# A two-layer attention and expert kernel: TensorE's groups of the first attention stage in another order

## The reference

```
x = x + _L0_xattn_ref(_layernorm(x), ctx, ctx, layer_indices, mask, ...)
q = split_heads(query @ Wq.T + bq) / sqrt(16)
k = split_heads(key @ Wk.T + bk)
v = split_heads(value @ Wv.T + bv)
scores = einsum('bhqd,bhkd->bhqk', q, k) + (1 - mask) * NEG
scores = where(same_layer_index, scores, NEG)
attn = softmax(scores)
ctx = einsum('bhqk,bhkd->bhqd', attn, v)
out = ctx @ Wo.T + bo
```

## Time and profile before

| what | value |
|---|---|
| median of three runs | 1462.81 us (1456.46 to 1464.56) |
| profiled execution: span | 1453.1 us |
| the runs above that span | 3.4 to 11.5 us, the median 9.7 |
| busy share of the span: TensorE matmuls, VectorE, ScalarE, GpSimd | 92%, 60%, 57%, 47% |
| first attention stage, b = 1 to 29, on TensorE's row | 33.08 to 350.39 us |

### The profile page before, as it was taken

The page is one execution under the profiler, slowest core; times in us unless marked ns, Lnnn a source line. Parts: engine busy times, 40 slices in busy tenths (PEclk is TensorE's granted clock), DMA queues, the critical chain, the costliest instruction groups (busy, mean ns, idle before and its releaser), DMA issues.

```text
span 1453.1 us, 37961 instructions
## 1 busy us (share of the span) xinstructions
PE 1337.7 (92%) x13114; PEld 1095.2 (75%) x13114; DVE 866.1 (60%) x2396; ACT 825.9 (57%) x1945; POOL 680.5 (47%) x939
## 2 busy tenths in 40 slices
PE   6999999997779999999997899999974999999997
PEld 5787777775546666666665799999963989889896
DVE  4787777877643333333332688888874666666664
ACT  4787777776345555555553566666643445444443
POOL 4235455455553333333331558778745344444323
PEclk8999999998789999999999899999996999999999
DMA  4344333332159999999996233333213433333331
GB/s 146 95 127 117 101 105 114 99 98 68 34 111 181 204 181 173 178 178 178 178 178 142 77 92 89 91 102 95 88 56 73 128 124 124 126 122 108 121 110 53
DMA packets 280922, 172.99 MB, mean 119 GB/s; under 512 B 213054, under 2 KB 259360, under 8 KB 280740
## 3 DMA queue, kind: packets, MB, share of 16 engines
q1 hardware_dynamic: 259156, 135.85, 39.6%
q0 software_dynamic: 18608, 32.21, 7.9%
q10 hardware_dynamic: 2976, 2.52, 0.6%
HBM read 93.44 MB, written 31.97 MB: 86 GB/s over the span
## 4 chain that ended last, share of the span: by engine, by line
PE 81%; DMA 4%; issue 4%; DVE 4%; ACT 3%; POOL 2%; another core or an unknown queue 1%; SPq 0%; ACTq 0%; DVEq 0%; POOLq 0%
PE psum L2424 14%; PE psum L1495 12%; PE psum L1475 12%; PE psum L2441 7%; PE psum L1996 3%; PE psum L901 2%; PE psum L1986 2%; PE psum L830 2%; PE psum L843 2%; PE psum L804 2%; PE psum L918 2%; PE psum L882 2%; PE psum L904 2%; PE psum L1906 2%; PE psum L1945 2%
## 5 line engine op out<-in xcount | busy, mean ns | idle before, releaser
L2424 PE MATMUL psum<-d_xT,d_w 128*128 128x256 f16 (+1 forms) x2304 | 228.7, 256 | 0.0
L2424 PEld LDWEIGHTS psum<-d_xT,d_w 128*128 128x128 f16 x2304 | 199.3, 98 | 19.0
L1395 DVE SCALAR_TENSOR_TENSOR b_h<-b_hid,b_h 128x1024 f16<-128x1024 f32 x71 | 87.0, 1225 | 211.2 <-ACT b_h L1430 207.9
L1475 PE MATMUL psum<-arena,b_xT 128*128 x852 | 197.2, 382 | 9.6 <-DMA b_xT<-b_x 7.9
L1495 PE MATMUL psum<-arena,b_hT 128*128 x1704 | 197.7, 273 | 3.4 <-DMA b_hT<-b_h 3.4
L1495 PEld LDWEIGHTS psum<-arena,b_hT 128*128 128x128 f16 x1704 | 166.0, 98 | 39.1 <-issue 5.7
L1305 POOL DMA_INDIRECT b_xg<-dram_normed,b_gi x71 | 69.6, 981 | 200.7 <-issue 128.3
L1475 PEld LDWEIGHTS psum<-arena,b_xT 128*128 128x128 f16 x852 | 83.7, 98 | 98.5 <-issue 14.8
L2505 ACT ACTIVATE d_sg<-psum 128x256 f32<-128x256 f32 (+1 forms) x192 | 66.0, 348 | 146.6 <-PE psum L2424 136.5
L2566 DVE SCALAR_TENSOR_TENSOR d_hf<-psum,d_sg 128x256 f32<-128x256 f32 (+1 forms) x192 | 71.1, 379 | 104.0 <-ACT d_sg L2505 85.9
L1423 ACT ACTIVATE b_hid<-psum 128x512 f32<-128x512 f32 x142 | 83.6, 596 | 67.5 <-PE psum L1475 59.6
(11 more groups left out here) (328 smaller groups left out, 3014.7 us busy)
## 6 DMA issues: line engine op xcount, KB each, us to landing
d_wst<-in_L_w SPq DMA_DIRECT2D x64, 384.0 KB
stage<-in_L_w SPq DMA_DIRECT2D x32, 512.0 KB
dram_expert_rows<-b_ys SPq DMA_DIRECT2D x71, 128.0 KB
ctxT<-in_ctxT SPq DMA_DIRECT2D x64, 128.0 KB
dram_normed<-xn SPq DMA_DIRECT2D x64, 128.0 KB
x<-in_x SPq DMA_DIRECT2D x32, 128.0 KB, 5.1
dram_x<-xnew SPq DMA_DIRECT2D x32, 128.0 KB
c_x<-dram_x SPq DMA_DIRECT2D x32, 128.0 KB
```

The costliest lines, as they stand in the source:

```text
L1395: dve.scalar_tensor_tensor(out=h16[:, p, 1, :], in0=hid[:, p, :], scalar=H_SCALE, in1=h16[:, p, 0, :], op0=ALU.mult, op1=ALU.subtract).the ...
L1475: i = pe.matmul(psum[:, 1 + 2 * p + half, :], xT[:, j % NT, px, c, :], weights(e, c, pw, half * 512, 512), start=(n == 0), stop=(n == len( ...
L2424: i = pe.matmul(psum[:, q, m * n:(m + 1) * n], w16[:, fc % RING, pw, col:col + P], xT[:, p, px, c, at:at + n], start=(k == 0), stop=(k == ...
```

## The change

`project_kv` is split in `project_k` and `project_v`. All the waits of `project_kv` stay with `project_k`, the signal `kv_done` with `project_v`. In TensorE's loop `project_k(b + 2)` moves ahead of `scores_t(b)`; `transpose_x1(b - 3)` moves ahead of `values(b - 1)`; `count` and `logits(b - 3)` move ahead of `transpose_x(b + 2)` and `transpose_back(b - 1)`. On ScalarE `x2T_out(b - 3)` moves ahead of `pvT_out(b - 1)`. Lines behind the split move by three: L904 becomes L907, L911 L914, L918 L921, L932 L935, L941 L944.

```diff
--- before.py
+++ after.py
@@ -751,8 +751,8 @@
                     k_out(b + 1)
                     v_out(b + 1)
                     q_out(b + 1)
+                    x2T_out(b - 3)
                     pvT_out(b - 1)
-                    x2T_out(b - 3)
                     high(b)
                     xnT_out(b + 2)
                     mT_out(b)
@@ -883,7 +883,7 @@
-                def project_kv(b):
+                def project_k(b):
                     if inside(b):
                         pe.wait_ge(ctx_ld[b % 2], nth(b))
                         if b == 0:
@@ -900,6 +900,9 @@
                             for c in range(DC):
                                 pe.matmul(psum[:, 1, o * P:(o + 1) * P], wk[:, c, o * P:(o + 1) * P], ctxT[:, b % 2, c, :],
                                           start=(c == 0), stop=(c == DC - 1))
+
+                def project_v(b):
+                    if inside(b):
                         for c in range(DC):
                             i = pe.matmul(psum[:, 1, 256:512], ctxT[:, b % 2, c, :], wv[:, c, :], start=(c == 0), stop=(c == DC - 1))
                         i.then_inc(kv_done, 1)
@@ -971,22 +974,23 @@
                 for b in range(-3, NB + 6):
                     scores(b)
+                    transpose_x1(b - 3)
                     values(b - 1)
-                    transpose_x1(b - 3)
                     unseen(b - 1)
-                    transpose_x(b + 2)
-                    transpose_back(b - 1)
                     if last_of(b - 4) is not None:
                         count(last_of(b - 4), b - 3)
                     logits(b - 3)
+                    transpose_x(b + 2)
+                    transpose_back(b - 1)
                     if b == NB:
                         turn_pe(pe, 0)
                         turn_pe(pe, 1)
                     if b in (NB + 1, NB + 2):
                         turn_pe(pe, b - NB + 1)
                     transpose_m(b)
+                    project_k(b + 2)
                     scores_t(b)
-                    project_kv(b + 2)
+                    project_v(b + 2)
                     transpose_o(b - 1)
                     if b == -2:
                         values_bias()
```

## The result

The changed kernel took 1479.62 us (median of four runs, 1473.86 to 1486.38); the kernel before, in four runs beside it, 1463.68. The ratio is 1.0132, 95% interval 1.0106 to 1.0157: 19 us slower by the ratio (the two medians lie 16 apart), where 27 were forecast. The profiled executions differ by 24.8 us in span.

The account below looks back on a forecast made before the run. TensorE's matmuls, busy for 92% of a 1453.1 us span, were taken as the bound. The terms summed to 27.4 us, a span of 1480.5; with the median run 9.7 us above the span, 1490 us was forecast, range 1480 to 1502.

Parts of the forecast that it names:

- the two ends: Start and end of the stage: 0.5 us added for each.
- The bound, and what pays for a wait: First attention stage: TensorE idles only some 14 us, so any wait added to it is paid almost one for one.
- The k projection leaves the cover: Before `project_o`, b = 1 to 28: less work hides ScalarE's exps and `attT`, a new wait of 0.88 us each.
- The wait for `mT` goes: Inside `scores_t`: `project_k` covers the wait, winning 0.17 us in early iterations and 0.04 later.
- A wait ahead of `project_k`: Between `transpose_m` and `project_k`: waits for `top` of some 0.2 us, or for `cnt_read` of 0.49 with a count.
- Rows ahead of values: On TensorE and ScalarE: the new order makes nothing wait, costed at nothing; without ScalarE's idle time, 0.27 us an iteration.
- The five longer iterations: b = 12, 16, 20, 24, 28: their longer period may take in the new waits, 0.4 us each, 2.0 together.
- More time at the lower clock: Rival: added TensorE idle time drops the clock in seven more iterations, 11.6 us on top, 1502 us; chance 0.08.
- The waits ahead of `project_k` do not show: Rival: `top` is through in time for `project_k`, taking off about 6 us, 1484 us; chance 0.08.
- Faster: Rival: ScalarE's exps could start 0.9 us earlier, so no wait before `project_o`, 4 us won, 1459 us; chance 0.03.

Follow-up runs that it names:

- e1: Changed kernel with only the split and the move of `project_k` kept, rows, values, logits and ScalarE's order put back; 1460.91 us, ratio 1.0231 to the kernel before.
- e8: Changed kernel with `project_v` moved ahead of `scores_t` as well; 1482.43 us, ratio 1.0383 to the kernel before.
- e11: Kernel before with `project_q` moved ahead of `scores_t`, `xnT_out` ahead of `high`, `attT` still after the fourth exp; 1442.71 us, ratio 1.0079 to the kernel before.
- e3: Changed kernel with `transpose_o` right behind `scores_t` and `attT` evicted after the second exp; 1428.98 us, ratio 1.0000 to the kernel before.
- e7: Kernel before with `transpose_o` right behind `scores_t` and `attT` evicted after the second exp; 1442.65 us, ratio 1.0087 to the kernel before.
- e2: Changed kernel with `project_kv` whole again at its old place, the new order of rows, values and logits kept; 1429.13 us, ratio 1.0000 to the kernel before.
- e10: Kernel before with `project_q` ahead of `scores_t`, then `project_k`, `transpose_o`, `project_v`, `attT` after the third exp, `xnT_out` ahead of `high`; 1422.11 us, ratio 0.9945.

## Why the prediction was right, point by point

**The number.** Its direction and its main term are shown below; that the size came out so close is in part luck. The span was forecast as 1480.5 us and is 1477.9. But of its growth, 24.8 us for the 27.4 forecast, the stage has 16.7 where the sum had 26.4, and the two ends have 3.5 and 4.6 where it had 0.5 each. With 0.5 and 0.1 at the ends on the experiments' chip, the change does not explain those 8 us. The other 8 us between 1490 and 1479.62 are the step from span to run: I carried over the 9.7 us by which the median run of before lay above its profiled span, and the median changed run lies 1.7 us above its own.

**The bound, and what pays for a wait.** Right on the experiments' chip, where the stage's growth is 29.2 of the 29.8 us between the spans; in the first pair it is 16.7 of 24.8. "Almost one for one" holds for the period, not for idle time, since 6.0 of those 29.2 us are recorded as busy time.

**The k projection leaves the cover, 0.88 us.** Right in place and mechanism, shown by e1 (all of the loss), e8 (twice the cover taken, 0.92 us more idle time), e11 (another group taken, the same 0.61 us) and e3 beside e7 (the wait taken away, the loss gone). Its size was 0.78 us and not 0.88, since `project_v` takes 0.97 from start to start when it follows `scores_t` and so covers more; 0.11 us come back at the next `scores`, since `project_o` comes without overlap after its wait. That is 0.89 together.

**The wait for `mT` goes, 0.17 early and 0.04 later.** Mis-sized: 0.55 in b = 4, and 0.43 in b = 14, where `scores_t` went from 178.28 - 176.38 = 1.90 us to 190.85 - 189.38 = 1.47. I read the wait off the idle time between matmuls. But a group that stalls in its middle shows most of that as busy time: the four `penalty` matmuls at 176.38 in the earlier trace rows are recorded as 0.82 us long without any idle time, and at 189.38, with `mT` ready, as 0.40. The measure is from start to start.

**A wait ahead of `project_k`, 0.2, with a count 0.49.** The wait is there. From `transpose_m` to `project_k` it added 0.26 us in b = 4, by 0.42 for 0.16, and 0.28 in b = 14, by 188.32 - 187.88 for 176.38 - 176.22. The group after a wait also loses its overlap, which e11 shows as 0.35. With a count the term was too large: b = 15 took 193.03 - 182.21 = 10.82 us before and 206.58 - 194.77 = 11.81 after, 0.99 more where 1.33 was forecast. In b = 14 the growth is 0.90 us where 1.03 was forecast (a period of 11.52 for 11.65): 0.88 for the lost cover, 0.28 for this wait, -0.43 for `mT`, and 0.17 for k and v, which take longer from start to start where they now stand and had no term. So a gain that I had nearly left out is partly made up by costs that I had too small or not at all.

**Rows ahead of values, nothing.** Right within what the ratio can tell: e2's is 1.0000. From `scores` to `transpose_m` b = 14 takes 4.63 us in both kernels (176.22 - 171.59 and 187.88 - 183.25), though the idle time recorded there went from 0.37 to 0.24.

**The five longer iterations, 0.4 us each.** Wrong in kind. I took them for a property of the order, and I overlooked b = 9, 17 and 25, which took 11.41, 11.24 and 11.25 us before and which I had as 10.62. In the profile of the kernel before on the experiments' chip none of the eight is longer than 10.54 us, and in the first profile of the changed kernel b = 12, 16, 20 and 24 take 11.6 us: b = 20 at 11.61 stands against the 12.78 of its kind. So some iterations got shorter, not longer, and the stage grew by 16.7 us in the first pair and by 29.2 in the second. That the latter is near the forecast of 27 is luck too: the common iteration grew by less than forecast (0.84 for 1.03 in b = 14), and some 4 us are the longer `mexp` of ten iterations, which no term had.

**The rivals.** More time at the lower clock: no, the stage's mean clock is 1.00 after, with 0.61 us of idle time before `project_o` in each iteration, and was 0.98 before. So the rule of the Trainium skill (Perfetto Trace Analysis, Matmul Optimizations) that the engine scales its power with utilisation does not tell these iterations apart; b = 12 before was idle for 12.78 - 11.76 = 1.02 us and had a mean clock of 0.87, b = 20 after was idle for 11.61 - 10.45 = 1.16 us at 1.00. What brings the lower clock about stays open; three iterations of e7 show it too. The waits ahead of `project_k` do not show: no, they do. Faster: no. The advice of the Trainium skill (Perfetto Trace Analysis, Optimization Strategy) is to find the gaps of the bounding engine and to make what they wait for start sooner or end faster. The change closed such a gap, the wait for `mT`, by other work, and that gave 0.55 us in b = 4, more than I allowed; the cover it took cost more.

## What to carry to other kernels

Before moving a group of work into a wait, look at what the group hides where it stands: sum the other engine's chain from its release to its use (here 2.80 us, and 0.05 to the start) against the work that stays behind it (2.97 with the group, 2.08 without). Pick for the gap the group with the fewest waits of its own, since it brings them along; `project_q` in the place of `project_k` was worth 0.4 us an iteration, though by itself it was still a loss against the kernel before (e11). And measure a suspected wait inside a run of matmuls from start to start against the same run without it, not by the idle time beside it.

## What was not expected of the hardware

The idle times between matmuls understate a wait: 0.17 us recorded and 0.55 lost for `mT`, 0.03 recorded and 0.3 lost for `attT` in e10.

A second is a small instruction's length. `mexp`, 128 x 16 elements, takes 0.23 us or 0.65 to 0.86, with some lengths between. In the traces of all runs it takes over 0.6 us 172 times. Each time GpSimd has an instruction under way when it starts, 168 times the indirect DMA (L569) and four times the `tensor_tensor` of L561, and in 163 of them `mexp` ends 0.02 to 0.04 us after that instruction; in the nine others, all b = 8, it ends 0.02 us before. In b = 12, before the change, VectorE and GpSimd (each from its own timeline):

```profile
150.69 0.25 DVE L1058 TENSOR_SCALAR mexp<-mx,negrow 128x16 f16<-128x16 f32 x1
```

```profile
151.66 1.08 POOL L569 DMA_INDIRECT dram_ids<-pairs,gsidx  x1 [0.17 <-issue]
```

and in the changed kernel on the same chip:

```profile
160.52 0.77 DVE L1062 TENSOR_SCALAR mexp<-mx,negrow 128x16 f16<-128x16 f32 x1
```

```profile
160.17 1.08 POOL L569 DMA_INDIRECT dram_ids<-pairs,gsidx  x1 [0.17 <-issue]
```

There `mexp` ends at 161.29, 0.04 us after the indirect DMA's 161.25. The Trainium skill, SBUF — State Buffer, Who interferes with whom, says that a `tensor_scalar` can enter a mode that needs the port pair which VectorE shares with GpSimd, and that the one issued later is then blocked until the other is through; the ends of the two agree with it. The changed kernel has 22 of 32 over 0.6 us, the one before 13, on the same chip. The iterations in which it became long grew by about 0.4 us more than the others, which no term of the sum had. That the one is the cause of the other was not tried by itself: no run moved the indirect DMA.
